# Moving a VectorE sum within its step and a product of values behind the V projection, in a cross-attention kernel on one core

## The reference, cut to what matters

```python
q = (scale * (Q @ Wq + bq)).reshape(bs, q_len, NH, DM)
k = (K @ Wk + bk).reshape(bs, kv_len, NH, DM)
v = (V @ Wv + bv).reshape(bs, kv_len, NH, DM)
qk = jnp.einsum('nlhd,nshd->nhls', q, k)
a = jax.nn.softmax(qk, axis=-1)
o = jnp.einsum('nhls,nshd->nlhd', a, v).reshape(bs, q_len, NH * DM)
return o @ Wo + bo
```

## Time and profile before

| | |
|---|---|
| median of three runs | 1455.58 us (1455.2 to 1456.13) |
| the profiled execution | 1453.62 us, its span 1451.9 us |
| PE busy | 1335.9 us, 92% |
| DVE busy | 1026.6 us, 71% |
| ACT busy | 890.0 us, 61% |
| POOL busy | 622.0 us, 43% |

### The profile page before, as it was taken

How to read it: one execution, slowest core, us unless ns; L and a number is a source line. 1 busy time by engine, 2 the same in 40 slices (tenths; PEclk the granted TensorE clock), 3 DMA queues, 4 the chain that set the end, 5 groups by cost and what they waited for, 6 DMA issues and landing times. The chain is left out here.

```text
span 1451.9 us, 24781 instructions
## 1 busy us (share of the span) xinstructions
PE 1335.9 (92%) x9380; PEld 1133.0 (78%) x9380; DVE 1026.6 (71%) x1407; ACT 890.0 (61%) x1716; POOL 622.0 (43%) x749
## 2 busy tenths in 40 slices
PE   5899999999999999999999999999999997489857
PEld 4788888888888887878888888888888886267734
DVE  3666677767766777667766776677668766389666
ACT  2667666666666666666666666766666664146521
POOL 5355545454545454545555454545454440000000
PEclk9999999999999999999999999999999999599979
DMA  4010000000001011100000000000000000300000
GB/s 124 16 44 2 15 1 9 8 16 1 8 9 30 1 37 30 37 30 1 8 21 3 1 9 16 8 1 8 8 1 1 1 9 1 98 1 1 1 1 14
DMA packets 25940, 22.95 MB, mean 16 GB/s; under 512 B 5472, under 2 KB 25568, under 8 KB 25824
## 3 DMA queue, kind: packets, MB, share of 16 engines
q1 hardware_dynamic: 25824, 21.39, 5.0%
HBM read 20.86 MB, written 0.52 MB: 15 GB/s over the span
## 5 line engine op out<-in xcount | busy, mean ns | idle before, releaser
L540 ACT ACTIVATE pT_hi<-psT 128x512 fp32r<-128x512 f32 x512 | 292.2, 598 | 220.6 <-PE psT L313 198.9
L615 DVE TENSOR_TENSOR pT_lo<-psT,pT_hi 128x512 fp32r<-128x512 f32 x512 | 338.6, 688 | 100.9 <-ACT pT_hi L540 83.6
L609 DVE TENSOR_REDUCE negm<-psS 128x1 f32<-128x1024 f32 x256 | 311.9, 1219 | 26.8 <-PE psS L303 26.8
L264 POOL TENSOR_TENSOR kT<-kraw,khi 64x512 fp32r<-64x512 f32 x252 | 324.6, 1288 | 0.0
L258 POOL CAST khi<-kraw 128x512 fp32r<-128x512 f32 x126 | 77.2, 613 | 523.2 <-ACT kraw L516 522.8
L506 ACT ACTIVATE prob<-psS,negm 128x1024 f32<-128x1024 f32 x256 | 285.8, 1117 | 1.0 <-DVE negm L609 1.0
L313 PE MATMUL psT<-ident,prob 128*128 128x128 f32 x2048 | 268.3, 274 | 3.9 <-DVE pT_lo L615 3.9
L329 PE MATMUL psO<-pT_hi,v 128*128 128x256 f32 x1024 | 267.3, 293 | 1.2 <-DVE pT_lo L615 0.4
L313 PEld LDWEIGHTS psT<-ident,prob 128*128 128x128 f32 x2048 | 234.2, 140 | 33.7 <-issue 7.1
L330 PE MATMUL psO<-pT_lo,v 128*128 128x256 f32 x1024 | 255.6, 282 | 0.0
L303 PE MATMUL psS<-kT,q_hi 64*128 64x512 f32 x1024 | 194.6, 417 | 3.3 <-ACT prob L506 2.0
(11 more groups left out here) (213 smaller groups left out, 1581.8 us busy)
## 6 DMA issues: line engine op xcount, KB each, us to landing
cst<-in_ctx_dram SPq DMA_DIRECT2D x12, 512.0 KB, 3.8
oT<-in_ctx_dram SPq DMA_DIRECT2D x4, 512.0 KB, 5.0
wraw<-in_L_xattn_Wk_dram SPq DMA_DIRECT2D x8, 256.0 KB, 2.6
wraw<-in_L_xattn_Wv_dram SPq DMA_DIRECT2D x8, 256.0 KB, 3.0
wraw<-in_L_xattn_Wq_dram SPq DMA_DIRECT2D x8, 256.0 KB, 2.7
wo<-in_L_xattn_Wo_dram SPq DMA_DIRECT2D x8, 256.0 KB, 2.8
ff_wdn<-in_L_ffn_w_down_dram SPq DMA_DIRECT2D x1, 704.0 KB, 8.0
ff_win<-in_L_ffn_w_gate_dram SPq DMA_DIRECT2D x1, 640.0 KB, 5.6
```

What stands on the lines that cost most here:

```text
L264: pool.tensor_tensor(kT[half, m // 2 % KRING, h, 1, :], raw[own, :], khi[own, :].bitcast(F32), ALU.subtract).then_inc(k_split, 1)
L540: act.activation(pT_hi[:, i % PRING, :], psT[:, t % 2, :], ACT.Copy).then_inc(ph_ok, 1)
L609: dve.tensor_reduce(negm[:, g % 2, h, qt, c:c + 1], psS[:, qt, :], AX.X, ALU.max, negate=True)\
L615: dve.tensor_tensor(pT_lo[:, i % PRING, :], psT[:, t % 2, :], pT_hi[:, i % PRING, :].bitcast(F32), ALU.subtract).then_inc(pl_ok, 1)
```

## The change

Two moves, and no instruction is added, removed or altered. VectorE's `add_out` goes from behind `v_low` to a place behind the second `maximum` of the same step, ahead of `p_low(n, 2)`. On TensorE, in context steps alone, `values(n, 1)` goes from ahead of the wait for `kraw_ok` and the V projection to a place behind the projection.

```diff
                 turn(n, 3)
+                early = prep_unit(n) is not None
                 values(n, 0)
-                values(n, 1)
+                if not early:
+                    values(n, 1)
                 if n + LEAD < N:
                     wait(pe, kraw_ok, n + LEAD + 1)
                     project_v(n + LEAD, psW[:, :])
+                if early:
+                    values(n, 1)
                 values(n, 2)
                 values(n, 3)
...
                 p_low(n, 1)
                 if n + 1 < N:
                     maximum(n + 1, 1)
+                if k < 8 and g >= 1:
+                    add_out(g - 1, k)
                 p_low(n, 2)
                 p_low(n, 3)
                 if n + LEAD < N:
                     v_low(n + LEAD, psW[:, :])
-                if k < 8 and g >= 1:
-                    add_out(g - 1, k)
```

## The result

| | before | after |
|---|---|---|
| median of four runs each | 1455.39 us (1453.55 to 1456.13) | 1441.05 us (1439.45 to 1442.6) |
| profiled execution, its span | 1453.62 us, 1451.9 us | 1441.08 us, 1439.4 us |
| PE busy | 1335.9 us, 92% | 1336.4 us, 93% |
| DVE busy | 1026.6 us, 71% | 1025.7 us, 71% |

The ratio is 0.9903, with a 95% interval from 0.9886 to 0.992: 14.3 us less, where 15.3 were forecast. TensorE's busy time moved by 0.5 us only; what went is the time in which it stood still.

The account below looks back on a forecast made before the run. TensorE was taken to pace the kernel. Gains of 8.8 us (merge steps) and 6.5 us (context steps), 15.3 in all, took the median from 1455.58 to 1440.3 us; range 1435.5 to 1447, the forecast's own 1438 to 1442.5.

Parts of the forecast that it names:

- TensorE paces the step, and only its standing still is worth anything: Whole kernel: TensorE, busy 1335.9 of 1451.9 us, sets the pace; moves elsewhere gain only what it stands still for.
- The merge step, 0.21 in 42 steps: Merge steps: moving add_out lets weigh_out start 0.21 us earlier, when the four post transposes end; 8.8 us in all.
- the first steps of the groups and the steps 49 to 55: Merge steps forecast to gain nothing: small weight operations, or prep_low in steps 49 to 55, stand ahead of the maximum.
- The context step, 0.27 in 24 steps: Context steps: V projection 0.47 us earlier, but v_high and the transpose only 0.27, limited by ScalarE; 6.5 us in all.
- The new place costs nothing: Behind the second maximum: add_out delays low parts, but the fourth product of values needn't wait; cost nothing.
- the pessimistic sum: At add_out's new place: fourth low part done by 219.90 at the latest, weights load at 220.03, so 0.13 us cover.
- a late low part in 56 steps, or in 48: Beyond the cover: each 0.1 us costs 0.1 in 56 steps, less in 8 of them; the slower rival counted 48.
- The sign that it named: A wait of the products of values (L329) for the low parts (L615) would show the forecast wrong.
- The rival of GpSimd and VectorE holding each other back: At add_out's new place: GpSimd's casts hold it by one cast (0.6 us), 22.6 us lost, time 1463; chance 3%.
- the K projection's wait for `weigh_out` to fall from 23.6 to about 15 us: Merge steps: a sign of the forecast, the wait of the K projection's weight loads dropping to about 15 us.
- its slices may fall differently: End of the kernel: low-clock slices may fall a little differently, since the gate's window runs freely; no size was given.

Follow-up runs that it names:

- the products in all steps: The changed kernel with the second product of values behind the V projection in all 128 steps, not in context steps alone: 1444.79 us, ratio 0.9921.
- the sum alone: The kernel before with only VectorE's add_out moved as in the change, the products of values in their old order: 1445.23 us, ratio 0.9939.
- the split of the scores: The changed kernel with a step's extra job between the two halves of the scores, except where the step before is a context step: 1449.58 us, ratio 0.9965.
- 512 more: The changed kernel with one more VectorE reduction, of 512 numbers into an unused tile, behind each moved add_out in the loop: 1457.12 us, ratio 1.0022.
- 128 more: The changed kernel with one more VectorE reduction, of 128 numbers into an unused tile, behind each moved add_out in the loop: 1442.23 us, ratio 0.991.
- the weights ahead: The changed kernel with VectorE computing the weights ahead of v_low in a group's last step, except context step n = 63: 1440.12 us, ratio 0.9891.
- the values alone: The kernel before with only values(n, 1) moved behind the V projection in context steps, add_out at its old place: 1447.57 us, ratio 0.9949.

## Why the prediction was right

- *TensorE paces the step, and only its standing still is worth anything.* Right: its busy time is the same, and a move that took no wait away (the products in all steps) gave 0.5 us at most in 104 steps.
- *The merge step, 0.21 in 42 steps.* Right in mechanism and size: from the first turn to the K projection 0.22 less, and the 42 steps give 8.9 us with the sum alone, 8.5 with both moves, where 8.8 were forecast. The next thing late was the end of the transposes, as said; the split of the scores shows it. That the first steps of the groups and the steps 49 to 55 gain nothing from the sum's move held too: with the sum alone none of them changed by more than 0.03. In the steps 49 to 55 VectorE still goes from `prep_low` to the maximum, 0.61 apart (502.82, 503.43).

```profile
502.82 0.69 DVE L636 TENSOR_TENSOR ctxT_lo<-psW,ctxT_hi 128x512 fp32r<-128x512 f32 x1 [1.44 <-ACT ctxT_hi L538]
503.43 1.21 DVE L613 TENSOR_REDUCE negm<-psS 128x1 f32<-128x1024 f32 x1
```

- *The context step, 0.27 in 24 steps.* Right, in 22 of them in full: 0.83 became 0.55, and ScalarE's exp was the limit. The emptied K projection didn't hold the V projection; its release arrived within the 0.11 between 89.65 and the weights load at 89.76.
- *The new place costs nothing.* Right: the rows of the changed kernel have 0.22 of cover where the pessimistic sum had 0.13, and the kernels with 512 and 128 more put its end at 0.17, between the two. What lies beyond it was sized too widely: the prediction charged a late low part in 56 steps, or in 48, and the kernel with 512 more paid in 42. The sign that it named, a wait of L329 for the low parts, has to be read beside the kernel before, which has 2.6 us of it already; that row didn't change.
- *The rival of GpSimd and VectorE holding each other back.* The sum ran from 215.92 to 217.01, beside two casts of GpSimd (from 215.84 and from 216.51, 0.61 each), and took 1.09 where it had taken 1.08 at its old place, so it wasn't held. The figure of the Trainium skill (VectorE: DVE Perf Modes, the TRN2 errata), an estimated 0.59 us for such an operation, differs from both rows. The same section of the Trainium skill adds that this figure comes out short for a single operation, with a measured fixed part of some 150 cycles; that would be an estimated 0.69 us, near the 0.67 that the reduction of 512 contiguous numbers took and far from the sum's 1.09. The measurement decides: by the figure of 0.59 the low parts would hardly have been put off, and they were by 0.54 (1.61 behind the second maximum's start before, 2.15 after).
- *A wait row that seems to have been misjudged.* I expected the K projection's wait for `weigh_out` to fall from 23.6 to about 15 us, and the row fell to 7.8 (14 times: the first steps of the groups and the steps 49 to 55). But the 0.15 that is left in each of the 42 steps, 6.3 us, is too short for a row, and with it the wait is 14.1 us. The forecast of the wait was right and the reading of the row was the trap: a row that vanishes from a list isn't a wait that is gone.
- *A term left out.* The time fell by 14.3 where 15.3 were forecast, and the profiled execution by 12.5. In the steps it was 14.9. The end stage, of which I had said only that its slices may fall differently, took 1.4 us more in the profiled execution. That the median came within 0.8 us of the forecast 1440.3 is in part luck: the trace can't say how much of this stage's time each of the other runs had.

## What to carry to other kernels

An operation that nobody waits for soon belongs behind the last operation that somebody does wait for, at a place where the engine would idle anyway; read its new cover from the next consumer's start, since an engine busy 71% of the time can have 0.2 us of slack at one place and none beyond. When a wait is shortened, work out what is late next before multiplying: here the moves were worth 0.22 of 0.32 and 0.28 of 0.71, and a further move paid only where it took away more than it added. For gains under half a per cent, measure a stretch that repeats, between the first and the last start of one operation, beside the whole time.

## What the hardware showed that wasn't expected

The stage behind the cross-attention has the same instructions in all these kernels, yet its length isn't the same. The stretch from VectorE's last operation of the cross-attention (which adds its output to `y`, at 1248.03 in the kernel before) to the end, one window each, of before, after, the sum alone, all products moved, and the weights ahead (window, its length, busy time of PE, PEld, DVE, ACT, POOL with counts, mean granted clock, DMA share, GB/s):

```profile
1248.00:1451.90 203.90, 155.45 (x764) 114.32 (x764) 139.75 (x248) 78.75 (x215) 1.50 (x6) 0.87 0.07 21
```
```profile
1234.10:1439.40 205.30, 157.19 (x764) 116.25 (x764) 139.72 (x248) 78.69 (x215) 1.50 (x6) 0.86 0.07 20
```
```profile
1239.80:1449.00 209.20, 162.34 (x764) 120.85 (x764) 139.64 (x248) 78.61 (x215) 1.50 (x6) 0.82 0.07 20
```
```profile
1234.00:1442.90 208.90, 162.32 (x764) 120.88 (x764) 139.70 (x248) 78.65 (x215) 1.50 (x6) 0.82 0.07 20
```
```profile
1229.50:1438.50 209.00, 161.22 (x764) 119.91 (x764) 139.85 (x248) 78.50 (x215) 1.50 (x6) 0.83 0.07 20
```

The same 764 matmuls are busy for 155 us at a mean granted clock of 0.87 and for 162 us at 0.82, and the stage is 203.9 or 209.2 us long. VectorE's busy time is the same to 0.2 us. So some 5 us hang on which stretches of this stage TensorE gets at 1.2 GHz and which at 2.4 GHz. In front of the stage TensorE idles while the last outputs are merged: in the kernel before it is busy for 1.8 us of the 4 from 1228, 1.5 of the next 4 and none of the 4 after those, at mean granted clocks of 1.00, 0.76 and 0.50. The level falls there in each of the kernels; how long it stays low differs. The differences go with the kernel in part (runs of the values alone lie within 2.0 us, all at a mean clock of 0.974) and with the execution in part: the kernel with the weights ahead has runs of 1441.6 us at 0.966 and of 1434.08 us at 0.973. The Trainium skill (TensorE: Matmul & The Clock Gate, Part 1) says that the gate's window runs freely, not tied to the kernel's start; executions of one kernel that differ fit that, but no run here shows the window itself. What sets the share of each case wasn't tried, and it stays open.
